# Four adjacency and kernel-matrix layers on one core: one product moved in front of a set of transposes, and a product group split in two

## The chip, the cores and the metric

The kernel runs on one core of a Trainium2 chip. The metric is device time in microseconds (us), the median over runs. Before the change it was 1554.31 us (three runs, 1549.61 to 1554.51 us).

Five engines run their own instruction queues and meet only through semaphores: TensorE (PE, matrix products; its weight loads are listed as PEld), VectorE (DVE), ScalarE (ACT), GpSimd (POOL) and SyncE (SP), which issues the transfers here.

## The reference

`x` is 64 x 128 x 512 (batch b, row l, column n), `adj` is 128 x 128. Four layers follow each other, each as `x = layernorm(x + layer(x))` over the last axis:

```
L0, L2 (ada_gcn):  x_norm = xn / |xn|;  S = sum over b, l of x_norm x_norm^T / B   (512 x 512)
                   keep the 153 largest entries of each row but its own, A = kept S, An = D^-1/2 A D^-1/2
                   out = An^T . (xn . adj) + bias
L1 (two kernels):  z_l = h W_lang^T, z_g = h W_grav^T, v = h W_V^T          (per batch, 128 x 512)
                   A_l = relu(cosines of z_l) , A_g = exp(-|z_g_i - z_g_j|^2 / 2 sigma^2), no diagonal
                   K = w_l rownorm(A_l * adj) + (1 - w_l) rownorm(A_g * adj)
                   out = (K v) W_O^T
L3:                out = (adj * adj)^T x + bias
```

## The kernel before, in words

The program has three parts. The first computes the 512 x 512 similarity of L0. The second builds its adjacency and then runs the middle stage: L0 and L1 of every batch (`gnn_layer_pair`). While that runs it also starts on the similarity of L2. The third part runs L2 and L3 (`last_layers`).

The change touches the middle stage only. It takes the 64 batches in 16 groups of four. Every product is done in three passes over a high and a low part of its operands (hi x hi, hi x lo, lo x hi), so after each product ACT rounds the result out of the accumulator bank (`y_hi`) and DVE writes the remainder (`y_lo`).

One turn of the stage works on three groups at once, in each engine's own written order:

- part A, group `ga`: the four first-layer products `l0(i)` (L1064, 12 matmuls of 512 columns each), the residual and statistics on DVE (`residual_a`, `stats_a`), `norm_a` on ACT, and `hturn(i)`, four transposes for each batch (L1047).
- part B, group `g`: four pairs `yprod(c)` (L1083), one half for `u_lang` and one for `u_grav`, with 6, 12, 18 and 24 matmuls for c = 0 to 3; the metric products `mprod(c)` (L1096) and value products `vprod(i)` (L1110), then transposes of the metrics. On DVE `diagonals` (L1546) takes the diagonals of the metrics once `mprod(3)` is done. ACT and DVE then need them for `v_hi(1)`, `ht_hi(0)` and `ht_lo(0)`, and `hturn(2)` on PE waits for `ht_lo(0)`, since it writes the same bank.
- part C, group `gp`: `k_turned` (L1138, four transposes of the finished kernel matrix `k_g`), its rounding `kt_hi` (ACT) and `kt_lo` (DVE), the four last-layer products `l1(i)` (L1150, 3 matmuls each), `residual_b(i)` (L1613), `stats_b(i)` and `norm_b(i)`.

Waits that matter below: `k_turned` waits for DVE's `kernel_sum` (L1602). `l1(0)` waits for `kt_hi` and `kt_lo`. `l1(2)` and `l1(3)` wait for `residual_b(0)` and `residual_b(1)`, which empty their banks. `yprod(c)` waits half by half for `y_lo(c-1)`. `mprod(0)` waits for all four `residual_b`. On POOL, `root_a(i)`, `root_b(i)` (L817, L819) give the inverse roots for the norms, and from the fifth full turn on `add_round` (L1470, L1474) adds three or four 128 x 512 tiles of squares for the next similarity, behind `root_a(3)`. On ACT `norm_b(0)`, `norm_b(1)` and `norm_a(0)` stand in front of `y_hi(2)`, and `norm_b(2)`, `norm_b(3)` and `norm_a(1)` in front of `y_hi(3)`. On DVE `stats_b(0)` and `stats_b(1)` stand in front of `y_lo(2)`; `stats_b(2)`, `stats_b(3)` in front of `y_lo(3)`, and that in front of `residual_a(3)`, which feeds `root_a(3)`.

There are 14 turns with all three parts (13 in a hardware loop, one behind it), then one with B and C (`nearly`), then one with C alone. The order within a turn is written out by hand, and the queue of each engine is strict.

Of the kernel before, what the change touches and what calls it, by code (L numbers as in the profile page):

```python
# [797 lines left out]
def first(g):  # L798
    return isinstance(g, int) and g == 0


def statistics(nc, dve, y, stats, mean_var, var_eps, neg_mean, y_ok, stats_ok, n, passed):

    dve.wait_ge(y_ok, n)
    nc.vector.bn_stats(stats, y).then_inc(stats_ok, 1)
    dve.wait_ge(stats_ok, 3 * n - 2)
    own_step(dve, passed)
    nc.vector.bn_aggr(mean_var, stats).then_inc(stats_ok, 1)
    dve.wait_ge(stats_ok, 3 * n - 1)
    nc.vector.tensor_scalar(var_eps, mean_var[:, 1:2], LN_EPS, None, ALU.add)  # L810
    nc.vector.tensor_scalar(neg_mean, mean_var[:, 0:1], -1.0, None, ALU.mult).then_inc(stats_ok, 1)  # L811
# [21 lines left out]
def gnn_layer_pair(nc, s, sb, sem, banks, adj, x, xw_dram, x_loaded, xw_in, out, u_l, u_g, wov):  # L833
# [112 lines left out]
    def sums_columns(k):  # L946

        return (banks[6][:, (k % 2) * CH * BLOCK:(k % 2 + 1) * CH * BLOCK] if k < 2 else factor_bank(k)[:, 0:CH * BLOCK])
# [88 lines left out]
    def tensor(pe):  # L1037
        def turn(gp, g, ga, following):
# [11 lines left out]
            def l0(i):  # L1050

                pe.wait_ge(xw_hi_ok, GRP * ga + i + 1)
                pe.wait_ge(xw_lo_ok, GRP * ga + i + 1)
                if i >= 2:
                    pe.wait_ge(ya_ok, GRP * ga + i - 1)
                elif not first(ga):
                    pe.wait_ge(ht_lo_ok, GRP * ga + i - 1)
                xwp, anp = (xw_hi, xw_lo), (an_hi, an_lo)
                for c in range(CH):
                    if first(ga) and i == 0:  # L1060
                        pe.wait_ge(adj.an_hi_ok, c + 1)
                        pe.wait_ge(adj.an_lo_ok, c + 1)
                    for n, (a, b) in enumerate(HILO):
                        mm = nc.tensor.matmul(l0_ps[i % 2][:], xwp[a][:, i % 2, c * P:(c + 1) * P], anp[b][:, c, :],  # L1064
                                              start=(c == 0 and n == 0), stop=(c == CH - 1 and n == 2))
                mm.then_inc(l0_made, 1)

            def yprod(c):

                if first(g) and c == 0:  # L1070
                    pe.wait_ge(adj.w_lo, 3 * CH)
                if c == 0:
                    pe.wait_ge(ht_hi_ok, GRP * (g + 1))
                    pe.wait_ge(ht_lo_ok, GRP * (g + 1))
                for k, u in enumerate((u_l, u_g)):
                    if c == 0:
                        pe.wait_ge(v_lo_ok, GRP * (g + 1) - 1 + k)
                    else:
                        pe.wait_ge(y_lo_ok, 8 * g + 2 * (c - 1) + k + 1)
                    for r in range(c + 1):  # L1080
                        for n, (a, b) in enumerate(HILO):
                            at = TRI[r] + (c - r) * P
                            mm = nc.tensor.matmul(yp[k][:], u[a][:, at:at + P],  # L1083
                                                  ht[b][:, r, :, :].rearrange("p i n -> p (i n)"),
                                                  start=(r == 0 and n == 0), stop=(r == c and n == 2))
                    mm.then_inc(y_made, 1)

            def mprod(c):

                pe.wait_ge(y_hi_ok, 8 * g + 2 * (c + 1))  # L1090
                pe.wait_ge(y_lo_ok, 8 * g + 2 * (c + 1))
                if c == 0:
                    pe.wait_ge(yb_ok, GRP * (g + 1))
                for i in range(GRP):
                    for n, (a, b) in enumerate(HILO):
                        mm = nc.tensor.matmul(mp[i // 2][:, (i % 2) * 256:(i % 2) * 256 + 256], ht[a][:, c, i, :],  # L1096
                                              y[b][:, c % 2, i, :, :].rearrange("p k n -> p (k n)"),
                                              start=(c == 0 and n == 0 and i % 2 == 0),
                                              stop=(c == CH - 1 and n == 2), skip_group_check=True)
                mm.then_inc(m_made, 1)  # L1100
# [34 lines left out]
            def k_turned():  # L1135
                pe.wait_ge(k_ok, GRP * (gp + 1))
                for i in range(GRP):
                    mm = nc.tensor.transpose(tr[0][:, i * P:(i + 1) * P], k_g[:, i, :], s.ident[:])  # L1138
                mm.then_inc(kt_made, 1)

            def l1(i):
                if i == 0:
                    pe.wait_ge(kt_hi_ok, gp + 1)
                    pe.wait_ge(kt_lo_ok, 1 + gp + 1)
                if i and last:
                    pe.wait_ge(yb_ok, GRP + GRP * gp + i)
                elif i >= 2:
                    pe.wait_ge(yb_ok, GRP + GRP * gp + i - 1)
                for n, (a, b) in enumerate(HILO):
                    mm = nc.tensor.matmul(tr[0][:] if last else mp[i % 2][:], kt[a][:, i, :], v[b][:, i, :], start=(n == 0), stop=(n == 2))  # L1150
                mm.then_inc(l1_made, 1)

            def block_sums(k):

                pe.wait_ge(added, GRP + BLOCK * (k + 1))
                if k >= 2:
                    pe.wait_ge(sums.normed, BLOCK * (k - 1))
                at = sums_columns(k)
                for c in range(CH):
                    mm = nc.tensor.matmul(at[:, c * BLOCK:(c + 1) * BLOCK], acc[:, k % 3, c * P:(c + 1) * P],  # L1160
                                          s.part_of[BLOCK][:], start=True, stop=True)
                mm.then_inc(n2_ok, 1)
# [11 lines left out]
            A, B, C = ga is not None, g is not None, gp is not None  # L1174
            last, nearly = C and not B, B and C and not A
# [23 lines left out]
                block_sums(0)  # L1199
            if B:  # L1200
                yprod(0)
            if C:
                k_turned()
            if nearly:
                block_sums(1)
                yprod(1)
            if A:
                l0(1)
            if C:
                l1(0)  # L1210
                l1(1)
            if B and not nearly:
                yprod(1)
            if C:
                l1(2)
                l1(3)
            if B:
                yprod(2)
                mprod(0)
            if A:  # L1220
                l0(2)
# [283 lines left out]
    def vector(dve):  # L1505
        def lo_part(lo, full, hi, done):
            nc.vector.tensor_tensor(lo, full, hi.bitcast(F32), ALU.subtract).then_inc(done, 1)  # L1507

        def turn(gp, g, ga, following):
# [8 lines left out]
            def residual_a(i):  # L1518
                dve.wait_ge(l0_made, 2 + GRP * ga + i + 1)
                if not first(ga) or i >= 2:  # L1520
                    dve.wait_ge(xa_ok, GRP * ga + i - 1)
                dve.wait_ge(x_loaded[i], 16 * (ga + 1))
                nc.vector.scalar_tensor_tensor(out=ya[:, i % 2, :], in0=l0_ps[i % 2][:], scalar=s.b0[:, 0:1],
                                               in1=xin[:, i, :], op0=ALU.add, op1=ALU.add).then_inc(ya_ok, 1)

            def stats_a(i):
                j = slice(i % 2, i % 2 + 1)
                statistics(nc, dve, ya[:, i % 2, :], st_a[:, i % 2, :], mv_a[:, i % 2, :], ve_a[:, j], nm_a[:, j],
                           ya_ok, st_a_ok, GRP * ga + i + 1, passed)

            def y_lo(c):
                for k in range(2):
                    dve.wait_ge(y_hi_ok, 8 * g + 2 * c + k + 1)
                    lo_part(y[1][:, c % 2, :, k, :], yp[k][:].rearrange("p (i n) -> p i n", i=GRP),
                            y[0][:, c % 2, :, k, :], y_lo_ok)
# [69 lines left out]
            def kt_lo():  # L1605
                dve.wait_ge(kt_hi_ok, gp + 1)
                lo_part(kt[1][:].rearrange("p i n -> p (i n)"), tr[0][:], kt[0][:].rearrange("p i n -> p (i n)"), kt_lo_ok)
# [26 lines left out]
            A, B, C = ga is not None, g is not None, gp is not None  # L1634
            last, nearly = C and not B, B and C and not A
# [41 lines left out]
                residual_a(0)  # L1677
            if B:
                y_lo(0)
            if C:  # L1680
                kt_lo()
            if nearly:
                invert(0, 2)
            if A:
                stats_a(0)
            if C:
                residual_b(0)
                residual_b(1)
            if A:
                residual_a(1)  # L1690
            if B:
                y_lo(1)
            if C:
                residual_b(2)
                residual_b(3)
            if A:
# [415 lines left out]
```

## Time and profile before

| | value |
|---|---|
| median of three runs | 1554.31 us |
| the profiled execution, its own time | 1555.39 us |
| its span (first to last instruction) | 1553.7 us |
| PE busy | 1429.7 us (92%) |
| DVE busy | 1203.3 us (77%) |
| ACT busy | 804.7 us (52%) |
| POOL busy | 542.2 us (35%) |
| middle stage, first to last full turn | about 334 to 1020 us of the span |

Busy times of a matmul overlap: a 512-column one is shown as 0.39 us long but the next starts 0.227 us later. So how long PE really stood still is best read from the starts of its instructions; the idle time in brackets in a row is smaller than that.

### The profile page before, as it was taken

Reading aid. Unit: us, or ns where it says so; the run is one execution under the profiler, and the core shown is the slowest. Engines: PE = TensorE matmul, PEld = TensorE weight load, DVE = VectorE, ACT = ScalarE, POOL = GpSimd, SP = SyncE. Lnnn points to the kernel's source line nnn. Section 1 sums busy time; section 2 is a strip of 40 time slices with the busy share of each in tenths; the row PEclk is TensorE's granted clock in tenths of the full one; section 3 lists DMA queues with packets and bytes.
Section 4 is the critical chain, followed back from the end, with each engine's and each line's share of the span. In section 5 each row is a group of like instructions: output and inputs, shape, how many; then the busy total and the mean of one; then the engine's idle time right before and its main releaser. Section 6 shows DMA issues by size and latency. Waiting matters only on the chain. (4 is left out here: it accounts for less than half of the span.)

```text
span 1553.7 us, 26749 instructions
## 1 busy us (share of the span) xinstructions
PE 1429.7 (92%) x7544; PEld 1199.4 (77%) x7544; DVE 1203.3 (77%) x3045; ACT 804.7 (52%) x1435; POOL 542.2 (35%) x740
## 2 busy tenths in 40 slices
PE   6998996899999999999999999998998945999996
PEld 5887875688888888888887888877887844777774
DVE  5987997566677766777667776667896996999997
ACT  5754552345434454445545455454553522777775
POOL 5950010112221133223331233322330002999996
PEclk9999997899999999999999999999999976999998
DMA  9803953212221222312232122315603840444443
GB/s 363 286 4 109 404 210 105 66 30 82 74 76 38 81 96 87 101 68 81 74 108 94 62 94 74 125 46 217 217 1 96 242 129 21 137 141 149 142 141 108
DMA packets 88025, 185.60 MB, mean 119 GB/s; under 512 B 9888, under 2 KB 10016, under 8 KB 86432
## 3 DMA queue, kind: packets, MB, share of 16 engines
q1 hardware_dynamic: 87968, 184.92, 34.5%
q8 instruction: 27, 0.44, 0.1%
q14 instruction: 30, 0.25, 0.0%
HBM read 134.55 MB, written 50.33 MB: 119 GB/s over the span
## 5 line engine op out<-in xcount | busy, mean ns | idle before, releaser
L817 POOL TENSOR_TENSOR rs_a<-ve_a,neghalf 128x1 f32<-128x1 f32 x64 | 40.1, 627 | 413.8 <-DVE nm_a L811 413.8
L1110 PE MATMUL bank<-wov,ht_hi 128*128 128x512 f32 x512 | 161.9, 397 | 0.0
L229 PE MATMUL bank<-xn_lo,xn_hi 128*128 128x512 f32 (+1 forms) x640 | 154.5, 373 | 7.6 <-DVE v_lo L1507 4.0
L1507 DVE TENSOR_TENSOR y_lo<-bank,y_hi 128x512 fp32r<-128x512 f32 x128 | 84.1, 687 | 87.3 <-ACT y_hi L1254 87.2
L207 ACT ACTIVATE xn_hi<-xn 128x512 fp32r<-128x512 f32 x128 | 80.8, 631 | 98.0 <-DVE xn L200 74.9
L1932 POOL TENSOR_TENSOR xw_lo<-xres,xw_hi 128x512 fp32r<-128x512 f32 x64 | 82.8, 1295 | 126.0 <-ACT xw_hi L1893 126.0
L212 DVE TENSOR_TENSOR xn_lo<-xn,xn_hi 128x512 fp32r<-128x512 f32 x128 | 116.1, 907 | 9.5 <-ACT xn_hi L207 9.3
L1254 ACT ACTIVATE y_hi<-bank 128x512 fp32r<-128x512 f32 x128 | 70.4, 585 | 101.9 <-PE bank L1083 97.6
L1317 ACT ACTIVATE xo<-xo,nb_b,rs_b 128x512 f32<-128x512 f32 x64 | 52.1, 815 | 132.9 <-POOL nb_b L819 132.9
L220 PEld LDWEIGHTS bank<-xn_hi 128*128 128x128 f32 x512 | 96.7, 193 | 19.4 <-ACT xn_hi L207 1.7
L1083 PE MATMUL bank<-ht_hi,u_lang 128*128 128x512 f32 x320 | 110.8, 395 | 0.8 <-issue 0.7
L1869 PE MATMUL bank<-an_hi,xw_hi 128*128 128x512 f32 x256 | 105.7, 413 | 4.0 <-ACT an_hi L703 2.9
L1083 PE MATMUL bank<-ht_hi,u_grav 128*128 128x512 f32 x320 | 109.2, 390 | 0.0
L1064 PE MATMUL bank<-an_hi,xw_hi 128*128 128x512 f32 x256 | 103.5, 404 | 5.3 <-ACT an_hi L703 2.9
L536 DVE MATCH_REPLACE8 work<-best,work 128x520 f32<-128x520 f32 x160 | 108.2, 683 | 0.0
L229 PEld LDWEIGHTS bank<-xn_lo,xn_hi 128*128 128x128 f32 x640 | 96.0, 195 | 15.4 <-DVE v_lo L1507 4.1
L1110 PEld LDWEIGHTS bank<-wov,ht_hi 128*128 128x128 f32 x512 | 91.8, 189 | 16.1
L1064 PE MATMUL bank<-an_lo,xw_hi 128*128 128x512 f32 x256 | 101.8, 398 | 0.0
L1064 PE MATMUL bank<-an_hi,xw_lo 128*128 128x512 f32 x256 | 101.7, 397 | 0.0
L1869 PE MATMUL bank<-an_hi,xw_lo 128*128 128x512 f32 x256 | 101.7, 397 | 0.0
L1869 PE MATMUL bank<-an_lo,xw_hi 128*128 128x512 f32 x256 | 100.8, 394 | 0.0
L1110 PE MATMUL bank<-wov,ht_lo 128*128 128x512 f32 x256 | 100.2, 391 | 0.0
(225 smaller groups left out, 3978.9 us busy)
## 6 DMA issues: line engine op xcount, KB each, us to landing
xw_dram<-stage SPq DMA_DIRECT2D x64, 256.0 KB, 6.8
stage<-xw_dram SPq DMA_DIRECT2D x64, 256.0 KB, 2.7
stage<-in_x SPq DMA_DIRECT2D x64, 256.0 KB, 2.7
between<-xo SPq DMA_DIRECT2D x64, 256.0 KB, 2.0
xres<-between SPq DMA_DIRECT2D x32, 512.0 KB, 5.9
x_at<-between SPq DMA_DIRECT2D x64, 256.0 KB, 2.9
xin<-between SPq DMA_DIRECT2D x64, 256.0 KB, 2.7
out<-xo SPq DMA_DIRECT2D x64, 256.0 KB, 2.0
```

Of the source, the lines that this page charges most:

```text
L207: self.nc.scalar.activation(self.hi[:, i % 4, :], self.xn[:, i % 4, :], ACT.Copy).then_inc(self.hi_ready, 1)
L212: self.nc.vector.tensor_tensor(self.lo[:, i % 4, :], self.xn[:, i % 4, :], self.hi[:, i % 4, :].bitcast(F32), ALU.subtract).then_inc(self. ...
L220: self.nc.tensor.matmul(self.at.hh[c], h[:, c * P:(c + 1) * P], h[:, c * P:N], start=(i == 0 and c < 3), stop=False, skip_group_check=True)
L229: mm = self.nc.tensor.matmul(out, h[:, c * P:(c + 1) * P], l[:, a:b], start=(i == 0 and c != 1), stop=False, skip_group_check=True)
L536: nc.vector.match_replace(work[:, c, :], best[:, c, :], work[:, c, :], CHOSEN).then_inc(marked[p], 1)
L1064: mm = nc.tensor.matmul(l0_ps[i % 2][:], xwp[a][:, i % 2, c * P:(c + 1) * P], anp[b][:, c, :], start=(c == 0 and n == 0), stop=(c == CH - ...
L1083: mm = nc.tensor.matmul(yp[k][:], u[a][:, at:at + P], ht[b][:, r, :, :].rearrange("p i n -> p (i n)"), start=(r == 0 and n == 0), stop=(r ...
L1110: mm = nc.tensor.matmul(yp[i % 2][:], ht[a][:, c, i, :], wov[b][:, c, :], start=(c == 0 and n == 0), stop=(c == CH - 1 and n == 2))
L1254: copy = lambda o, i: nc.scalar.activation(o, i, ACT.Copy)
L1507: nc.vector.tensor_tensor(lo, full, hi.bitcast(F32), ALU.subtract).then_inc(done, 1)
L1869: mm = nc.tensor.matmul(l2_ps[i % 2][:], xwp[a][:, i % 2, c * P:(c + 1) * P], anp[b][:, c, :], start=(c == 0 and n == 0), stop=(c == CH - ...
L1932: nc.gpsimd.tensor_tensor(xw_lo[:, i % 2, :], of_batch(ga, i), xw_hi[:, i % 2, :].bitcast(F32), ALU.subtract).then_inc(xw_lo_ok, 1)
```

## The change

On PE, `l0(1)` moves in front of `k_turned`, and `yprod(1)` right behind `k_turned`. `l1(0)` and `l1(1)` follow, then the `u_lang` half of `yprod(2)`, then `l1(2)` and `l1(3)`, then the `u_grav` half. DVE's order follows: `stats_a(0)` and `residual_a(1)` stand in front of `kt_lo`, and `y_lo(1)` in front of the four `residual_b`. ACT's, POOL's and SP's orders stay as they were. In the turn with B and C only, `l0` is absent, so there only the split of `yprod(2)` and DVE's order differ.

```diff
-            def yprod(c):
+            def yprod(c, of=(0, 1)):
...
-                for k, u in enumerate((u_l, u_g)):
+                for k in of:
+                    u = (u_l, u_g)[k]
...
             if B:
                 yprod(0)
+            if A:
+                l0(1)
             if C:
                 k_turned()
             if nearly:
                 block_sums(1)
+            if B:
                 yprod(1)
-            if A:
-                l0(1)
             if C:
                 l1(0)
                 l1(1)
-            if B and not nearly:
-                yprod(1)
+            if B:
+                yprod(2, (0,))
             if C:
                 l1(2)
                 l1(3)
             if B:
-                yprod(2)
+                yprod(2, (1,))
                 mprod(0)
...
             if B:
                 y_lo(0)
+            if A:
+                stats_a(0)
+                residual_a(1)
             if C:
                 kt_lo()
             if nearly:
                 invert(0, 2)
-            if A:
-                stats_a(0)
+            if B:
+                y_lo(1)
             if C:
                 residual_b(0)
                 residual_b(1)
-            if A:
-                residual_a(1)
-            if B:
-                y_lo(1)
-            if C:
                 residual_b(2)
                 residual_b(3)
```

PE's queue in the loop's turn, around the transposes of `k_g`, before. ISA and REGISTER_ALU rows are waits and counters, not work; bank_23 holds `l0(1)`, bank_27 the `u_grav` half of a `yprod`.

```order
L1083 MATMUL bank_27<-ht_hi_1956,u_grav_34_54 128x512
L1136 ISA
L1138 MATMUL bank_30<-ident,k_g_1966 128x128 x4
L1052 REGISTER_ALU
L1064 MATMUL bank_23<-an_hi_1943,xw_hi_1953 128x512
```

And now (the lines of the code have moved by one):

```order
L1064 MATMUL bank_23<-an_hi_1943,xw_hi_1953 128x512
L1064 MATMUL bank_23<-an_lo_1944,xw_hi_1953 128x512
L1064 MATMUL bank_23<-an_hi_1943,xw_lo_1954 128x512
L1137 ISA
L1139 MATMUL bank_30<-ident,k_g_1966 128x128 x4
L1080 ISA
L1084 MATMUL bank_26<-ht_hi_1956,u_lang_31_51 128x512
```

The twelve matmuls of `l0(1)` have moved from behind the transposes to before them, and `yprod(1)` stands behind them.

PE's queue at `l1(3)` (bank_24, the second of the two banks for the last layer) before, with `yprod(2)` whole behind it:

```order
L1150 MATMUL bank_24<-v_hi_1969,kt_hi_1967 128x512
L1150 MATMUL bank_24<-v_lo_1970,kt_hi_1967 128x512
L1150 MATMUL bank_24<-v_hi_1969,kt_lo_1968 128x512
L1079 REGISTER_ALU
L1083 MATMUL bank_26<-ht_hi_1956,u_lang_31_51 128x512
```

And now, where bank_26 is the `u_lang` half and bank_27 the `u_grav` half:

```order
L1084 MATMUL bank_26<-ht_hi_1956,u_lang_32_52 128x512
L1149 ISA
L1151 MATMUL bank_25<-v_hi_1969,kt_hi_1967 128x512
L1151 MATMUL bank_25<-v_lo_1970,kt_hi_1967 128x512
L1151 MATMUL bank_25<-v_hi_1969,kt_lo_1968 128x512
L1149 REGISTER_ALU
L1151 MATMUL bank_24<-v_hi_1969,kt_hi_1967 128x512
L1151 MATMUL bank_24<-v_lo_1970,kt_hi_1967 128x512
L1151 MATMUL bank_24<-v_hi_1969,kt_lo_1968 128x512
L1080 REGISTER_ALU
L1084 MATMUL bank_27<-ht_hi_1956,u_grav_33_53 128x512
```

`l1(2)` and `l1(3)` now stand behind nine matmuls of `yprod(2)` that used to follow them, and only nine instead of 18 stand between `l1(3)` and `mprod(0)`.

DVE's queue before, from the end of the second `y_lo` pair (`y_lo(1)`) on; xo is `residual_b`:

```order
L1523 SCALAR_TENSOR_TENSOR stage_49<-bank_23,b_8,stage_49 128x512
L1533 REGISTER_ALU
L1507 TENSOR_TENSOR y_lo_1959<-bank_26,y_hi_1958 128x4x128
L1533 REGISTER_ALU
L1507 TENSOR_TENSOR y_lo_1959<-bank_27,y_hi_1958 128x4x128
L1611 REGISTER_ALU
L1613 TENSOR_TENSOR xo_1971<-bank_25,xb_1964 128x512
L1611 REGISTER_ALU
L1613 TENSOR_TENSOR xo_1971<-bank_24,xb_1964 128x512
L1507 TENSOR_TENSOR xw_lo_1954<-stage_49,xw_hi_1953 128x512
L805 BN_STATS st_b<-xo_1971 128x6
```

And now:

```order
L1525 SCALAR_TENSOR_TENSOR stage_49<-bank_23,b_8,stage_49 128x512
L1509 TENSOR_TENSOR kt_lo_1968<-bank_30,kt_hi_1967 128x512
L1535 REGISTER_ALU
L1509 TENSOR_TENSOR y_lo_1959<-bank_26,y_hi_1958 128x4x128
L1535 REGISTER_ALU
L1509 TENSOR_TENSOR y_lo_1959<-bank_27,y_hi_1958 128x4x128
L1613 REGISTER_ALU
L1614 REGISTER_ALU
L1615 TENSOR_TENSOR xo_1971<-bank_25,xb_1964 128x512
L1613 REGISTER_ALU
L1615 TENSOR_TENSOR xo_1971<-bank_24,xb_1964 128x512
```

`kt_lo` has moved behind `residual_a(1)` (stage from bank_23), and all four `residual_b` stand behind `y_lo(1)`; two more xo rows, `xw_lo` and the first `stats_b` follow as before.

## Rows read from the trace of the kernel before

**Rows 1.** The page: busy time per engine, and the clock granted to TensorE in 40 slices.
```profile
PE 1429.7 (92%) x7544; PEld 1199.4 (77%) x7544; DVE 1203.3 (77%) x3045; ACT 804.7 (52%) x1435; POOL 542.2 (35%) x740
...
PEclk9999997899999999999999999999999976999998
```

**Rows 2.** Three single turns: window, length, busy time (count) by engine, clock, DMA.
```profile
430.34:478.64 48.30, 47.77 (x249) 40.57 (x248) 33.91 (x107) 22.72 (x44) 9.51 (x21) 1.00 0.21 65
...
526.94:575.50 48.56, 48.03 (x249) 40.49 (x248) 34.41 (x107) 24.66 (x48) 13.34 (x24) 1.00 0.26 87
...
625.15:674.79 49.64, 48.11 (x250) 40.48 (x248) 35.56 (x109) 24.67 (x48) 14.64 (x25) 1.00 0.26 85
```

**Rows 3.** PE's waits in 335 to 1003 us: total, times, longest.
```profile
PE bank L1138 <- DVE k_g L1602: 7.7, 14, 0.7
PE bank L1047 <- DVE ht_lo L1507: 5.9, 6, 1.0
```

**Rows 4.** PE in the turn that starts at 724.38: start, length, instruction, [idle <- releaser].
```profile
724.38 0.39 PE L1064 MATMUL bank<-an_hi,xw_hi 128*128 128x512 f32 x1
...
728.24 0.39 PE L1083 MATMUL bank<-ht_hi,u_grav 128*128 128x512 f32 x1
729.16 0.66 PE L1138 MATMUL bank<-ident,k_g 128*128 128x128 f32 x4 [0.53 <-DVE k_g L1602]
729.57 0.47 PE L1064 MATMUL bank<-an_hi,xw_hi 128*128 128x512 f32 x1
...
732.42 0.39 PE L1150 MATMUL bank<-v_hi,kt_hi 128*128 128x512 f32 x1
...
741.94 0.28 PE L1096 MATMUL bank<-y_hi,ht_hi 128*128 128x256 f32 x1
...
747.55 0.40 PE L1083 MATMUL bank<-ht_hi,u_lang 128*128 128x512 f32 x1
```

**Rows 5.** DVE in the same turn.
```profile
730.88 0.68 DVE L1507 TENSOR_TENSOR kt_lo<-bank,kt_hi 128x512 fp32r<-128x512 f32 x1
...
733.48 1.36 DVE L1613 TENSOR_TENSOR xo<-bank,xb 128x512 f32<-128x512 f32 x2 [0.74 <-PE bank L1150]
...
737.33 0.69 DVE L1507 TENSOR_TENSOR y_lo<-bank,y_hi 128x512 fp32r<-128x512 f32 x1 [0.59 <-ACT y_hi L1254]
737.93 1.28 DVE L1613 TENSOR_TENSOR xo<-bank,xb 128x512 f32<-128x512 f32 x2
...
745.13 1.29 DVE L1507 TENSOR_TENSOR y_lo<-bank,y_hi 128x512 fp32r<-128x512 f32 x2 [2.96 <-ACT y_hi L1254]
...
755.94 0.75 DVE L1523 SCALAR_TENSOR_TENSOR stage<-bank,b,stage 128x512 f32<-128x512 f32 x1 [1.12 <-PE bank L1064]
```

**Rows 6.** POOL's adds: a turn with four (from 674.79), one with three (from 724.38).
```profile
709.60 5.67 POOL L1474 TENSOR_TENSOR acc<-acc,sq 128x512 f32<-128x512 f32 x4
...
760.65 2.73 POOL L1474 TENSOR_TENSOR acc<-acc,sq 128x512 f32<-128x512 f32 x2
```

**Rows 7.** DVE's diagonals: a turn without adds (430.34), with four, with three.
```profile
468.61 0.29 DVE L1546 CUSTOM_DVE_ANT_0 a_l<-m,ident 128x128 f32<-128x128 f32 x1 [1.23 <-ACT m L1254]
...
714.05 1.35 DVE L1546 CUSTOM_DVE_ANT_0 a_l<-m,ident 128x128 f32<-128x128 f32 x1
...
762.67 0.87 DVE L1546 CUSTOM_DVE_ANT_0 a_l<-m,ident 128x128 f32<-128x128 f32 x1 [1.23 <-ACT m L1254]
```

**Rows 8.** PE at `hturn(2)` in the turn with four adds.
```profile
719.71 1.23 PE L1047 MATMUL bank<-ident,xa 128*128 128x128 f32 x8 [0.97 <-DVE ht_lo L1507]
```

**Rows 9.** The turn with parts B and C only (from 1019.70): PE, DVE, ACT, PE.
```profile
1030.21 0.39 PE L1150 MATMUL bank<-v_hi,kt_hi 128*128 128x512 f32 x1
...
1033.57 1.28 DVE L1613 TENSOR_TENSOR xo<-bank,xb 128x512 f32<-128x512 f32 x2
...
1039.11 1.09 ACT L1254 ACTIVATE y_hi<-bank 128x512 fp32r<-128x512 f32 x2 [0.17 <-PE bank L1096]
...
1040.48 0.50 PE L1083 MATMUL bank<-ht_hi,u_lang 128*128 128x512 f32 x1
```

## The prediction, on record before the changed kernel ran

> **What bounds the kernel now.** I read the page first. PE is busy 92% of the span and its clock is at the upper level, 2.4 GHz, in nearly every slice of the middle stage [rows 1], so time can only be won there where PE stands still. Next I cut the stage into turns. They come in three lengths: about 48.3 us for the four turns in which POOL adds no squares, 48.56 us with three adds, 49.64 us with four [rows 2]. PE's waits name two places [rows 3]: in all 14 full turns it waits at `k_turned` for DVE's `k_g`, and in six turns at `hturn(2)` for `ht_lo(0)`. Last come the timelines of one turn, to see what stands behind each wait.
>
> The real price of the first wait: the last matmul before it starts at 728.24 and a 512-column matmul takes a slot of 0.227 us (17 of them in 724.38 to 728.24), so PE was free at 728.46; the transposes start at 729.16 [rows 4]. PE loses **0.70 us per turn**, 9.8 us in 14 turns. That is all that the change can win in the full turns.
>
> **The change, step by step, in the turn from 724.38.** No instruction is added or removed. PE's new order gives, with 0.41 us for the transposes (729.16 to 729.57), 12 matmuls = 2.72 us, and 0.13 us lost behind transposes (the 12 matmuls from 729.57 took 2.85 us until 732.42) [rows 4]:
> `l0(1)` 728.46, `k_turned` 731.18 (its `k_g` is there since 729.16: no wait, 2.0 us to spare), `yprod(1)` 731.59, `l1(0)` 734.44, `l1(1)` 735.12, first half of `yprod(2)` 735.80, `l1(2)` 737.84, `l1(3)` 738.52, second half 739.20, `mprod(0)` 741.24, against 741.94 before. So the 0.70 us arrives at `mprod(0)`, if nothing is late on the way. What could be:
> - `kt_lo`, now behind `stats_a(0)` and `residual_a(1)`. `kt_lo` ran at 730.88, and DVE then needs 1.2 us for the statistics and 0.7 us for the residual, so `kt_lo` starts about 732.8 and ends 733.5, before `l1(0)` at 734.44. Covered by `yprod(1)`, with 0.9 us to spare; the cover gone, each us costs a us in 14 turns.
> - `y_lo(1)`: its second half started 3.55 us behind the start of `yprod(1)` (733.78, that is 732.42 and six slots; 737.33) [rows 4, 5]. Now that is 735.3, and the first half 1.3 us earlier; the halves of `yprod(2)` want them at 735.8 and 739.2. Covered.
> - `residual_b`: the first one starts 1.06 us behind the start of its `l1` (732.42, 733.48). Now `residual_b(0)` follows `y_lo(1)` at 735.9, done before `l1(2)` at 737.84; `residual_b(3)` starts at 738.52 + 1.06 = 739.58 and is done 1 us before `mprod(0)` needs it. Covered.
>
> **But the residuals are now later, and that is what I think matters.** `residual_b(3)` started at 737.93 + 0.60 = 738.53 and now starts at 739.58: **1.05 us later**. From there a chain runs without a gap: `xw_lo(2)`, `stats_b(0)`, `stats_b(1)`, POOL's roots, `norm_b(1)`, `norm_a(0)`, `y_hi(2)`, `y_lo(2)`. DVE waits 2.96 us in front of `y_lo(2)`, for ACT, which waits for POOL: that idle time is latency in this chain and not slack. It starts at 745.13 [rows 5]; now at 746.18, its first half done at 746.87. `yprod(3)` stood at 747.55 and is due at 746.85 [rows 4]. With a hand-over and an unhidden weight load it starts about 0.17 us late. So **0.53 us** of the 0.70 survive there. (From both sides: 0 if the hand-over is hidden, 0.3 if the load is paid in full and the chain is 0.1 us longer.)
>
> The chain goes on through `stats_b(3)`, `norm_b(3)`, `norm_a(1)`, `y_hi(3)` and `y_lo(3)` to `residual_a(3)` on DVE. There the row of before shows 1.12 us of idle time for PE [rows 5]. The chain is 1.05 us later: `residual_a(3)` is ready at 755.94 - 1.12 + 1.05 = 755.87. PE's side is ready at 755.94 - 0.53 = 755.41, so DVE is now the later one: `residual_a(3)` moves by only 0.07 us, while PE moves by 0.53.
>
> Who waits for that? POOL's adds stand behind the root that `residual_a(3)` feeds, and the adds hold up DVE. In a turn without adds the first diagonal takes 0.29 us. With adds it takes 0.87 us (762.67), and the third one in a four-add turn 1.35 us; each ends where an add ends (760.65 + 2.73 = 763.38; 709.60 + 5.67 = 715.27) [rows 6, 7]. From the diagonals the way leads to `ht_lo(0)` and `hturn(2)`, the second wait of PE: 0.97 us shown in the four-add turn [rows 8]; in the three-add turn it is just reached, as its length shows. So in **ten** turns the end is tied to POOL's last add, and that moves by 0.07 us.
>
> The Trainium skill ("SBUF — State Buffer", Who interferes with whom) says that a DVE instruction with two SBUF inputs contends with a GpSimd instruction that reads SBUF, and whoever issues first holds the pair for the whole instruction. The trace agrees as to the waiting, 0.29 against 1.35 us; it shows two diagonals getting through between two adds where the rule would let one through. By the rule the rival "between two adds" below would be worth half.
>
> **The turn with B and C only.** It has no `l0`, so nothing is won at its `k_turned`. `l1(3)` now stands 18 matmuls behind `l1(0)`: 1030.21 + 4.08 = 1034.29, `residual_b(3)` at 1035.35 instead of 1033.57 + 0.60 = 1034.17, 1.18 us later. ACT had 0.17 to 0.25 us of idle in front of `y_hi(2)`, waiting for PE; `yprod(3)` at 1040.48 already stood right behind `y_lo(2)` [rows 9]. So **0.95 us are lost** here, and nothing later in the program is seen to give them back.
>
> **The sum.** Four turns without adds x 0.53 = 2.1 us, the first of them waits 0.15 us longer and wins that too: 2.3. Ten turns with adds x 0.07 = 0.7. Minus 0.95. Net 2.0 us won. From the profiled execution's own 1555.39 us that gives 1553.4; that execution stands 1.1 us above the median, 1554.31, so I predict **1552.3 us**.
>
> **Rivals.**
> 1. *Between two adds.* The metrics are there at 762.67 - 0.53 = 762.14; the last add issues at 763.38 - 1.29 - 0.07 = 762.02. I have the diagonals 0.12 us too late. If `yprod(3)` does not wait (0.70 instead of 0.53), the first two diagonals pass ahead of the last add, and 0.43 us less stand behind it. Then ten turns win 0.50, four 0.70: 5.0 + 2.8 + 0.15 - 0.95 = 7.0, 1547.3 us. For it: 0.12 us is little. Against it: the hand-over costs something, and the rows repeat to 0.03 us from turn to turn.
> 2. *The whole wait is won.* 9.8 us, 1544.5. It needs the chain of the residuals to be shorter than I read it, or POOL's adds to move with PE. Against it the 1.12 us in [rows 5], all used up.
> 3. *Slower: the residual chain overtakes.* The point from which it decides is a shift of 1.12 us, where POOL's adds begin to come later than before; I reckon 1.05. At 1.6 us the adds are 0.48 us later in ten turns (4.8 lost), the turns without adds win nothing, the B-C turn loses 1.5: 1560.6. It needs DVE to reach the residuals 0.5 us later than computed; nothing in the rows says so.
> 4. *The wait only moves.* `kt_lo` comes too late and PE stands at `l1(0)` instead: 1554.3 to 1555.5. Against it the 0.9 us to spare.
>
> **Chances.** Forecast 0.58, rival 1 0.18, rival 2 0.08, rival 3 0.09, rival 4 0.07. About 0.3% (4.7 us) is what this measurement can tell from no change. Forecast and rival 4 lie within it, but for 0.05 (0.04 faster, 0.01 slower): faster 0.30, same 0.60, slower 0.10. The forecast's own range is 1550.3 to 1554.6. The range for all takes in rival 1 and the first half of rival 3: 1547.0 to 1556.5.
>
> **What the new profile would show.** No wait of PE at the transposes of `k_g` in the 14 turns. `residual_b(3)` about 15.2 us into a turn instead of 14.15. A short idle before `yprod(3)`. DVE's idle before `residual_a(3)` gone or charged to ACT. Turns of 47.8 us without adds, but 48.5 and 49.55 with them, and a longer wait at `hturn(2)` (about 1.5 us). In the B-C turn about 1 us of idle before `yprod(3)`. I am wrong if turns with four adds are shorter by 0.3 us or more, or if PE waits at `l1(0)` or at `mprod(0)`.

## The result, and the profile after

| | before | after |
|---|---|---|
| median (20 runs each) | 1554.05 us (1549.61 to 1557.37) | 1549.8 us (1548.58 to 1551.83) |
| ratio after / before | | 0.9976, 95% interval 0.9969 to 0.9984 |
| profiled execution: own time, span | 1555.39, 1553.7 us | 1549.01, 1547.3 us |

By the medians the change wins 4.25 us. The ratio says 0.24%, which is 3.7 us, and its interval reaches from 2.5 to 4.8 us. 1552.3 us was predicted, with 1547.0 to 1556.5 as the range for all cases. The direction and that range were right. But the measured median lies 0.5 us below the forecast's own range (1550.3 to 1554.6), and the gain is twice the 2.0 us that I had. It lies within 0.3%, as the likeliest case said, though the interval shows that it is no zero.

PE's waits after, 335 to 1003 us, to be read against [rows 3]: total, times, longest. It is the only one that the view lists.

```profile
PE bank L1047 <- DVE ht_lo L1509: 8.8, 9, 1.4
```

The wait for `k_g` is gone in all 14 turns, 7.7 us of it. The wait at `hturn(2)` has grown from 5.9 us in six places to 8.8 us in nine. The three kinds of turn after (window, length, busy time by engine, clock, DMA), against [rows 2]:

```profile
429.73:477.43 47.70, 47.70 (x250) 40.70 (x249) 33.92 (x107) 22.71 (x44) 9.49 (x21) 1.00 0.21 66
525.13:573.47 48.34, 48.05 (x250) 40.60 (x249) 34.78 (x107) 24.67 (x48) 13.33 (x24) 1.00 0.26 87
622.88:672.27 49.39, 48.07 (x249) 40.60 (x248) 35.89 (x109) 24.68 (x48) 14.63 (x25) 1.00 0.24 85
```

Without adds a turn is 0.60 us shorter, with three adds 0.22 us, with four 0.25 us. In the turns without adds PE now has no gap that the page shows at all (47.70 busy of 47.70).

The turn from 721.66 after, on PE (against [rows 4]):

```profile
721.66 0.39 PE L1064 MATMUL bank<-an_hi,xw_hi 128*128 128x512 f32 x1
...
728.47 0.60 PE L1139 MATMUL bank<-ident,k_g 128*128 128x128 f32 x4
728.83 0.48 PE L1084 MATMUL bank<-ht_hi,u_lang 128*128 128x512 f32 x1
...
744.15 0.50 PE L1084 MATMUL bank<-ht_hi,u_lang 128*128 128x512 f32 x1
```

The transposes come 6.81 us into the turn with no idle in front of them. `yprod(3)` comes at 22.49 us (744.15) instead of 23.17 (747.55 - 724.38). And on DVE (against [rows 5]):

```profile
736.12 1.37 DVE L1615 TENSOR_TENSOR xo<-bank,xb 128x512 f32<-128x512 f32 x2 [1.72 <-PE bank L1151]
737.40 0.68 DVE L1509 TENSOR_TENSOR xw_lo<-stage,xw_hi 128x512 fp32r<-128x512 f32 x1
...
743.41 1.29 DVE L1509 TENSOR_TENSOR y_lo<-bank,y_hi 128x512 fp32r<-128x512 f32 x2 [2.95 <-ACT y_hi L1256]
...
751.80 1.29 DVE L1509 TENSOR_TENSOR y_lo<-bank,y_hi 128x512 fp32r<-128x512 f32 x2 [0.91 <-ACT y_hi L1256]
753.00 0.74 DVE L1525 SCALAR_TENSOR_TENSOR stage<-bank,b,stage 128x512 f32<-128x512 f32 x1
```

`y_lo(2)` stands 21.75 us into the turn (20.75 before), and the 1.12 us of idle in front of `residual_a(3)` (the last row) have gone: it starts 31.34 us into the turn, right behind `y_lo(3)`. It was 31.56 before. Then POOL's adds and DVE's diagonals, in the turn with three adds (against [rows 6, 7]):

```profile
757.71 2.73 POOL L1476 TENSOR_TENSOR acc<-acc,sq 128x512 f32<-128x512 f32 x2
```

```profile
759.38 1.21 DVE L1548 CUSTOM_DVE_ANT_0 a_l<-m,ident 128x128 f32<-128x128 f32 x1 [1.23 <-ACT m L1256]
```

The adds end at 760.44, 38.78 us into the turn instead of 39.00. The diagonal starts 0.57 us earlier in its turn and takes 1.21 us instead of 0.87, so it ends only 0.23 us earlier, as the last add does. That is the gain being handed back.

### The profile page after: what moved, and what is told of

Same layout as the page of the kernel before. It is cut to its first block and busy times, and to the rows that moved or that the text cites. A ratio compares the mean times of both kernels' runs of the same rounds, so it can differ in the third digit from the quotient of the medians.

```text
span 1547.3 us, 26749 instructions
## 1 busy us (share of the span) xinstructions
PE 1428.4 (92%) x7544; PEld 1199.1 (77%) x7544; DVE 1206.2 (78%) x3045; ACT 804.5 (52%) x1435; POOL 542.0 (35%) x740
## 5 line engine op out<-in xcount | busy, mean ns | idle before, releaser
L817 POOL TENSOR_TENSOR rs_b<-ve_b,neghalf 128x1 f32<-128x1 f32 x64 | 34.8, 543 | 201.4 <-DVE nm_b L811 201.4
```

The lines of the kernel that those rows point to most:

```text
L817: nc.gpsimd.tensor_tensor(root, var_eps, neghalf, ALU.pow).then_inc(root_ok, 1)
```

## The experiments

Each ran beside the kernel before on the same chip; the ratio is to those runs, whose median was 1554.1 to 1555.6 us. "Turn" is the length of a turn without, with three and with four adds, from PE's starts in the profile.

| kernel | runs | median us | ratio to before (95%) | turn, us |
|---|---|---|---|---|
| before | 20 | 1554.05 | 1 | 48.3 / 48.56 / 49.6 |
| changed | 20 | 1549.8 | 0.9976 (0.9969 to 0.9984) | 47.7 / 48.34 / 49.4 |
| before, late adds | 5 | 1542.41 | 0.9926 (0.9912 to 0.994) | 48.3 / 48.3 / 48.3 |
| changed, late adds | 4 | 1534.87 | 0.987 (0.9854 to 0.9887) | 47.7 / 47.7 / 47.7 |
| changed, xw_lo(2) early | 5 | 1544.97 | 0.9934 (0.9919 to 0.9949) | 47.5 / 47.8 / 48.9 |
| changed, no split | 11 | 1558.1 | 1.0026 (1.0016 to 1.0036) | 48.5 / 48.8 / 49.8 |
| before, 0.6 us more in the chain | 12 | 1554.48 | 1.0006 (0.9993 to 1.0018) | 48.3 / 48.5 / 49.6 |
| changed, 0.6 us more in the chain | 6 | 1558.9 | 1.0035 (1.0021 to 1.0048) | 48.3 / 49.0 / 50.0 |
| changed, DVE's order as before | 2 | 1593.74 | 1.0259 (1.0236 to 1.0282) | 50.2 / 50.8 / 51.9 |
| changed, late adds, old B-C turn | 4 | 1536.73 | 0.9885 (0.9866 to 0.9904) | 47.7 / 47.7 / 47.7 |
| the same and xw_lo(2) early | 4 | 1533.33 | 0.9855 (0.9839 to 0.9871) | 47.5 / 47.5 / 47.5 |

**1 and 2. The adds behind the diagonals**, in the changed kernel (run 1) and in the one before (run 2). Is the gain lost to POOL's adds?

```diff
             root_a(3)
-            for r in rounds[:1]:
-                add_round(r)
...
                 nc.gpsimd.tensor_tensor(r_l[:], q_l[:], s.neghalf[:], ALU.pow).then_inc(r_ok, 1)
-            for r in rounds[1:]:
+            for r in rounds:
                 add_round(r)
```

> The changed kernel with one edit on POOL: in every turn the adds of the squares stand behind the inverse root r_l instead of in front of it, so no add runs while DVE takes the diagonals. Theory (the residuals' chain holds up POOL's adds, these hold up the diagonals, and so the gain is lost in the turns with adds): all 14 full turns get the length of a turn without adds, 47.7 us; against the changed kernel's 1549.8 that is 9 turns x 0.63 to 1.7 us plus 1.2 us in the fourteenth, about 13 us less: 1536.5. Rival (the limit of the turns with adds is ScalarE's load of squares or something else in them, not the place of the adds): turns of 48.3 and 49.4 us as now, 1549.8, or longer if the adds now meet the later two-input instructions of DVE.

> The kernel before with the same edit on POOL alone. Theory: all turns 48.3 us, 7 x 1.33 + 3 x 0.26 = 10 us less than before, 1544. The distance between this kernel and the changed one with late adds is then what the change is worth when nothing takes it back: about 14 x 0.6 less the loss in the turn with B and C only, 7.5 us, against 4.2 us measured without this edit. Rival (the change is worth the same 4 us wherever the adds stand): 4 us between the two.

Both came out 1.6 us better than expected, in the order expected. In the changed kernel a turn with three adds and one with four are now as long as the ones without:

```profile
428.31:476.02 47.71, 47.71 (x249) 40.69 (x248) 33.90 (x107) 22.73 (x44) 9.54 (x21) 1.00 0.19 66
523.72:571.42 47.70, 47.70 (x249) 40.69 (x248) 33.89 (x107) 24.81 (x48) 13.36 (x24) 1.00 0.26 88
571.42:619.11 47.69, 47.69 (x249) 40.69 (x248) 33.91 (x107) 24.82 (x48) 14.73 (x25) 1.00 0.25 88
```

ScalarE still squares (its 24.8 us against 22.7) and POOL still adds (14.7 us of work), so it was the place of the adds and nothing else in these turns. The edit also lets `r_l` run ahead of the adds, which could be a second cause. But before the edit `r_l` was not held by them: in the changed kernel's turn with three adds POOL waited 1.17 us for DVE's `q_l`, which DVE makes after the diagonal that is held, before it ran:

```profile
761.61 1.03 POOL L1499 TENSOR_TENSOR r_l<-q_l,neghalf 128x4 f32<-128x4 f32 x1 [1.17 <-DVE q_l L1553]
```

In the four-add turn with late adds the first diagonal takes 0.29 us again, and the adds follow:

```profile
609.15 0.29 DVE L1546 CUSTOM_DVE_ANT_0 a_l<-m,ident 128x128 f32<-128x128 f32 x1 [1.23 <-ACT m L1256]
```

```profile
611.44 5.60 POOL L1476 TENSOR_TENSOR acc<-acc,sq 128x512 f32<-128x512 f32 x4
```

With the adds late, the change is worth 1542.41 - 1534.87 = 7.5 us, as expected; with them early 4.25 us. So by whole runs the adds take back 3.3 us of it, by an edit that touches neither PE nor DVE. The profiles say it more sharply, since they leave out what differs outside the 14 full turns. From the first of these turns to the start of the B-C turn the change wins 4.9 us with early adds (1019.70 - 333.56 = 686.14 us, then 1015.56 - 334.30 = 681.26) and 8.8 us with late ones (1009.30 - 332.83 = 676.47, then 1000.54 - 332.91 = 667.63). There the adds take back 4.0 us.

**3. `xw_lo(2)` in front of `residual_b(2)`**: is the chain from the residuals what sets the place of the adds?

```diff
                 residual_b(1)
+            if A:
+                xw_lo_(2)
+            if C:
                 residual_b(2)
                 residual_b(3)
-            if A:
-                xw_lo_(2)
```

> The changed kernel with one edit on DVE: xw_lo(2) stands in front of residual_b(2) instead of behind residual_b(3), in DVE's idle gap. The adds stay where they are. It takes one instruction (0.6 us) out of the chain from residual_b(3) to residual_a(3). Theory: residual_a(3) then comes when PE allows it, 30.9 us into the turn instead of 31.34; the turns with adds become 0.4 us shorter (48.3 to 47.9, 49.4 to 49.0), those without stay at 47.7; ten turns, about 4 us less: 1545.7. Rival (chain not binding): no change, 1549.8.

1544.97 us, 4.8 us less than the changed kernel for moving one DVE instruction into a gap (5.9 us by the 14 full turns of the two profiles, 681.26 and 675.41 us). The turns with adds lost 0.5 us each, as the chain theory says. Those without lost 0.19 us, which I had not expected: it is the small wait that the chain still caused in front of `yprod(3)`, which shows no idle in a bracket. In the second full turn PE's starts of the two kernels agree up to there and are 0.07 us apart at the first matmul of `yprod(3)` and 0.18 to 0.19 us from the second on. The rows of the turns:

```profile
428.94:476.45 47.51, 47.51 (x249) 40.63 (x248) 33.96 (x108) 22.71 (x44) 9.51 (x21) 1.00 0.21 66
523.97:571.78 47.81, 47.81 (x249) 40.54 (x248) 34.48 (x107) 24.68 (x48) 13.34 (x24) 1.00 0.26 88
571.78:620.66 48.88, 47.87 (x249) 40.54 (x248) 35.62 (x109) 24.66 (x48) 14.70 (x25) 1.00 0.24 86
```

**4. Without the split.** What is the second part of the change for?

```diff
-            if B:
-                yprod(2, (0,))
             if C:
                 l1(2)
                 l1(3)
             if B:
-                yprod(2, (1,))
+                yprod(2)
                 mprod(0)
```

> The changed kernel with the third y whole behind the four last-layer products, as before the change; l0(1) still stands in front of the transposes, and DVE's order is the new one. Theory: l1(2) then waits for residual_b(0) (12.1 us into the turn, PE is there at 11.4) and l1(3) for residual_b(1); PE loses about 0.85 us of the 0.70 it won, and residual_b(3) is no later than before: every turn is 0.15 us longer than in the kernel before, 1556. So moving l0(1) without the split would win nothing. Rival (the split is only there to be tidy, the gain comes from l0(1)): 1549.8 or, as the residuals are earlier, down to 1546.

1558.1 us, slower than the kernel before. The wait at `k_g` has turned into one at `l1(2)` for `residual_b(0)`, 0.65 us, once in each of the 14 turns; `l1(3)` follows it without a gap:

```profile
PE bank L1151 <- DVE xo L1613: 9.1, 14, 0.7
PE bank L1047 <- DVE ht_lo L1507: 6.1, 6, 1.0
```

A turn without adds is 48.45 to 48.49 us against 48.3 before (0.15 us more expected, 0.14 to 0.18 measured), and the 14 turns together are 2.75 us longer. With this DVE order, moving `l0(1)` wins only together with nine matmuls between `l1(1)` and `l1(2)`. The reverse, the split alone with `l0(1)` in its old place, was not run.

**5 and 6. 0.6 us more in the residuals' chain**, in the kernel before (run 5) and in the changed one (run 6): how much room does each have?

```diff
             if A:
+                dve.wait_ge(xw_hi_ok, GRP * ga + 3)
+                dve.wait_ge(spare_ok, ga)
+                nc.vector.tensor_tensor(spare[:], xw[:, 0, :], xw_hi[:, 0, :].bitcast(F32),
+                                        ALU.subtract).then_inc(spare_ok, 1)
                 xw_lo_(2)
```

> The kernel before with one instruction more on DVE in each of the 14 full turns: a copy of the subtraction of xw_lo(2), 0.6 us, written to a spare tile, between residual_b(3) and stats_b(0). It lengthens the chain from the residuals to y_lo(2), y_lo(3) and residual_a(3) by 0.6 us and nothing else. Theory: in this kernel the chain has 0.67 us to spare in front of yprod(3) and 1.2 us in front of residual_a(3); no change, 1554.5 within 1 us. Rival (DVE is simply full, any instruction costs its length; or the turns are bound elsewhere): 14 x 0.6 = 8.4 us more, or the same small amount in both kernels.

> The changed kernel with the same extra instruction. Theory: the changed order has used up the room, so each of the 14 turns gets 0.6 us longer: 48.3 without adds, 48.9 and 50.0 with; 8.4 us more than 1549.8, 1558, that is slower than the kernel before. Rival (the residual chain binds nothing): no change, 1549.8.

The same instruction costs 0.4 us (nothing, by its interval) in the one and 9.1 us in the other (1558.9 - 1549.8); by the 14 full turns it is 0.2 and 8.8 us. Turns of the kernel before with it, then of the changed one:

```profile
428.96:477.28 48.32, 47.78 (x250) 40.55 (x248) 34.50 (x108) 22.73 (x44) 9.51 (x21) 1.00 0.20 65
...
623.77:673.40 49.63, 48.11 (x250) 40.47 (x248) 36.17 (x110) 24.68 (x48) 14.63 (x25) 1.00 0.25 85
```

```profile
430.52:478.80 48.28, 47.78 (x249) 40.70 (x248) 34.49 (x108) 22.73 (x44) 9.49 (x21) 1.00 0.20 65
...
626.12:676.12 50.00, 48.13 (x249) 40.60 (x248) 36.49 (x110) 24.68 (x48) 14.61 (x25) 1.00 0.25 84
```

DVE is busy 0.6 us more per turn in both (34.50 and 34.49 us against 33.9), so a full DVE isn't the reason. The chain has room in the kernel before and none in the changed one.

**7. PE's new order with DVE's old one.** Does DVE's part matter?

```diff
-            if A:
-                stats_a(0)
-                residual_a(1)
             if C:
                 kt_lo()
             if nearly:
                 invert(0, 2)
-            if B:
-                y_lo(1)
+            if A:
+                stats_a(0)
             if C:
                 residual_b(0)
                 residual_b(1)
+            if A:
+                residual_a(1)
+            if B:
+                y_lo(1)
+            if C:
                 residual_b(2)
                 residual_b(3)
```

> The changed kernel with DVE's order as before the change (kt_lo before stats_a(0), residual_b(0) and (1) before residual_a(1) and y_lo(1)); PE's order is the new one. Theory: kt_lo waits for the later transposes until 8.1 us into the turn, residual_b(0) for l1(0), and y_lo(1) comes at 13.0 instead of 9.5; the first half of yprod(2) waits for it, 2.4 us in each of 15 turns: about 35 us more than the changed kernel, 1585. Rival (PE's order alone is the change): 1549.8.

1593.74 us, 44 us more than the changed kernel instead of 35. PE stands for `y_lo(1)` as expected:

```profile
PE bank L1084 <- DVE y_lo L1509: 28.7, 13, 2.2
```

A turn without adds is 2.5 us longer (50.2), 14 of them are 35 us. But five of the turns took 1.6 us more than their kind, 8 us in all. There TensorE had fallen to its lower level, 1.2 GHz, behind the 2.2 us of standing still; a matmul's slot is 0.43 us in place of 0.227. Such a turn as a whole, with a mean granted clock of 0.97 (others of its kind take 50.8 us at 1.00), and then PE in it:

```profile
536.97:589.37 52.40, 49.90 (x249) 41.67 (x248) 34.79 (x107) 24.67 (x48) 13.34 (x24) 0.97 0.23 80
```

```profile
550.71 0.80 PE L1084 MATMUL bank<-ht_hi,u_lang 128*128 128x512 f32 x1 [2.21 <-DVE y_lo L1509]
551.30 0.63 PE L1084 MATMUL bank<-ht_lo,u_lang 128*128 128x512 f32 x1
551.73 1.06 PE L1084 MATMUL bank<-ht_hi,u_lang 128*128 128x512 f32 x2
```

**8. Late adds, and the old order in the turn with parts B and C only.** Does the change lose there?

```diff
-            if B:
+            if B and not nearly:
                 yprod(2, (0,))
...
-                yprod(2, (1,))
+                yprod(2, (0, 1) if nearly else (1,))
...
-            if B:
+            if B and not nearly:
                 y_lo(1)
             if C:
                 residual_b(0)
                 residual_b(1)
+            if nearly:
+                y_lo(1)
+            if C:
                 residual_b(2)
```

> The changed kernel with the late adds, and in the one turn with parts B and C only the old order on PE and DVE. Theory: the split costs 0.72 us there in front of yprod(3) and nothing is won there; so yprod(3) at 19.2 us of that turn where TensorE keeps its upper clock, 20.8 where it falls to the lower level for part of yprod(1), as in the kernel before; 0.5 to 0.9 us less than the late adds alone, 1534.1, inside the noise of the totals, to be read from the turn. Rival (the split helps there too): later than 19.9 or 21.5.

The total, 1536.73 us (1533.44 to 1537.51), can't be told from that of run 1 (1533.15 to 1537.44). The turn itself tells it. `yprod(3)` with the old order, then with the new one (both with late adds; these two B-C turns start at 1001.02 and 1000.54):

```profile
1021.80 0.50 PE L1084 MATMUL bank<-ht_hi,u_lang 128*128 128x512 f32 x1
```

```profile
1022.05 0.50 PE L1084 MATMUL bank<-ht_hi,u_lang 128*128 128x512 f32 x1 [1.19 <-DVE y_lo L1507]
```

That is 20.78 us into the turn with the old order and 21.51 with the new one: 0.73 us lost. In both, TensorE ran part of `yprod(1)` at the lower level. At the upper level it is 19.20 (before, late adds) against 19.92 (changed): 0.72.

**9. All edits that should help.** Run 8 with `xw_lo(2)` early as in run 3.

> The changed kernel with late adds, xw_lo(2) in front of residual_b(2), and the old order in the turn with parts B and C only. Theory: with the adds out of the way only a wait of 0.19 us in front of yprod(3) is left to the residuals' chain; xw_lo(2) early takes it away: all 14 full turns 47.5 us instead of 47.7, 2.7 us less than the late adds with the old order in that turn, 1534. Rival (the rest of the 0.7 us is lost elsewhere, in the transposes): turns stay at 47.7.

```profile
523.77:571.28 47.51, 47.51 (x249) 40.63 (x248) 33.97 (x107) 24.81 (x48) 13.33 (x24) 1.00 0.26 88
571.29:618.80 47.51, 47.51 (x250) 40.63 (x248) 33.98 (x107) 24.81 (x48) 14.69 (x25) 1.00 0.25 88
```

All 14 turns are 47.5 us, 2.5 us less in sum than in run 8 (2.7 expected). At 1533.33 us it is the fastest measured here, 1.45% under the kernel before; its distance from run 1 (1.5 us) is within the spread of both.

## Why the prediction was right, and where its size was off

**The wait at `k_g`.** 0.70 us per turn were to be won. Without the chain of the residuals (runs 3 and 9) a turn is 47.51 us against 48.31: 0.80 us. Of the 0.10 us more, 0.04 is there at `mprod(0)`: the transposes take 0.36 us (728.47 to 728.83) when they follow the stream instead of 0.41 us behind a stall. The other 0.06 us come in the last seventh of the turn, behind `hturn(0)`; what gives them stays open.

**The residuals 1.05 us later.** `y_lo(2)` is 1.00 us later, and so is `residual_b(3)`: it starts 0.60 us before `xw_lo(2)` (737.40), 15.14 us into the turn instead of 14.15. Right as mechanism and size; runs 5 and 6 show that this chain has become the one that counts.

**0.53 us left behind `yprod(3)`.** The turns without adds won 0.60 us: 0.55 us from the second matmul of `yprod(3)` on, and the rest behind it. Run 3 shows the 0.19 us that are lost there; 0.17 was my figure.

**0.07 us in the turns with adds: the term that was mis-sized.** The ten turns won 0.2 to 0.3 us each, 2.3 us instead of 0.7. The working was `residual_a(3)` ready at "755.94 - 1.12 + 1.05". Its 1.12 us is the idle time in the bracket of [rows 5], counted from the shown end of `y_lo(3)`. But a shown length overlaps the next start by 0.09 us: two `y_lo` fill 1.29 us on the page, and in the changed kernel the next instruction starts 1.20 us behind their start (751.80, 753.00). With 1.21 for 1.12 and 1.00 for 1.05 the same sum gives 0.21 us, and `residual_a(3)` moved by 0.22 (31.56 to 31.34). Ten turns turn an error of 0.15 us into 1.5 us, nearly all of the 1.65 us by which the turns with adds won more than predicted. That the adds are what ties these turns (runs 1 and 2), and the chain what places the adds (run 3), was right.

**The turn with parts B and C.** 0.95 us of loss predicted, 0.72 to 0.73 measured in front of `yprod(3)`. The profiled pair shows the opposite: the turn is 42.51 us after and 43.38 before. That is the clock and not the change: in run 5, whose code in this turn is that of before, TensorE kept its upper level and the turn took 41.81 us (1018.58 to 1060.39), 0.70 less than after. Granted clock over the 4.5 us from the start of `yprod(1)`, before and after:

```profile
1025.70:1030.20 4.50, 4.50 (x15) 3.62 (x15) 1.93 (x4) 0.66 (x2) 0.00 (x0) 0.63 0.00 0
```

```profile
1021.56:1026.06 4.50, 4.50 (x21) 3.72 (x22) 3.37 (x7) 1.25 (x3) 0.00 (x0) 1.00 0.00 0
```

**The sum.** Turns without adds 2.55 us (2.3 predicted), with adds 2.35 (0.7), B-C turn -0.7 (-0.95): 4.2 us, against 4.25 by the medians and 2.5 to 4.8 by the interval. That the two agree to 0.05 us is luck. The profiles of the kernel before and of run 5 have full turns of 686.14 and 686.35 us in sum, but spans of 1553.7 and 1549.2 us: 1.3 us of the difference lie in front of these turns, 1.6 in the B-C turn (its clock) and 1.8 behind it. So an execution's own time carries several microseconds that have nothing to do with the change; why the part in front and the part behind differ stays open.

**The rivals.** *Between two adds* did not happen: the diagonals came 37.72 us into the turn and the last add had begun at 37.48, so it held them. My distance of 0.12 us was 0.24, for the adds moved too. *The whole wait is won* is nearly what happens when the adds are out of the way: 8.8 of 9.8 us in the full turns, 7.5 us of the whole (runs 1 and 2). *The chain overtakes* is what 0.6 us more do: slower than before (run 6). *The wait only moves* is what happens without the split (run 4) or without DVE's part (run 7). The signs that I gave held for the most part: a wait at `hturn(2)` of 1.31 to 1.35 us in the turns with four adds (1.5 predicted), turns of 47.7, 48.34 and 49.4 (47.8, 48.5, 49.55), 1.17 us of idle before `yprod(3)` in the B-C turn (1), and no wait at `l1(0)` or `mprod(0)`. Only the short idle before `yprod(3)` in the full turns shows in no bracket.

By the Trainium skill ("SBUF — State Buffer", Who interferes with whom) a DVE instruction with two SBUF inputs and a GpSimd instruction that reads SBUF contend for a port pair that is an exclusive lock, and the order of issue decides which of them is blocked. The traces agree: the same diagonal takes 0.29 us with no add beside it (run 1) and 1.21 us with one (the changed kernel). Which add it meets was decided by the place of an instruction on another queue.

## What to carry to other kernels

A wait that is removed by moving other work in front of it makes that work's neighbours later; follow what they release to the end of the loop body, over every engine, before the wait is counted as won. Idle time in front of an instruction that waits for another engine's answer to one's own work is part of a chain and not room; room is only where the waiting engine and the answer are independent. And where two engines hold each other up without a semaphore, look at which of them could do its work in a gap: here moving three or four adds won more than twice what the reordering did.

## What the runs showed of the hardware that I had not expected

- TensorE's clock fell behind a stall in some executions and not in others. In the B-C turn PE stands still for 1.6 us in front of the transposes of `k_g` in every kernel, and in the 3 us before that it ran only small matmuls of 16 columns and six of 512; the 12 matmuls of `yprod(1)` behind the transposes then took 4.2 to 4.4 us, most of them at 1.2 GHz, in the profiles of six kernels (a mean granted clock of 0.62 to 0.64 over 4.5 us) and 2.85 us at 2.4 GHz in those of five. With DVE's old order it fell in five of 14 turns behind 2.2 us of standing still. A single pair of profiles can differ by 1.6 us through this alone (`yprod(3)` 20.79 us into the turn in the kernel before, 19.22 in run 5).
- Apart from that, turns of one kind repeat to 0.07 us within a profile, but for the first and the last of the 14. So an effect of 0.2 us per turn can be read from one profile, while whole runs of one kernel spread over 2 to 8 us.
- The extra DVE instruction in the kernel before left the turns at the same length to 0.04 us (but for the last, 0.2 us longer), though DVE is busy 70% of a turn (33.9 of 48.3 us).
